# The linear stage's rounds: the place of the mask, of the second norm and of the gathers

## The reference

```python
qkv = x @ W_qkv.T
q, k, v = (to_heads(t) for t in jnp.split(qkv, 3, axis=-1))      # 16 heads of 8
q = softplus(q / norm(q)); k = softplus(k / norm(k))
kv = einsum('bhnd,bhnc->bhdc', k, v) * 8 ** -0.5
ksum = sum(k, axis=2) + 1e-6
out = einsum('bhnd,bhdc,bhn->bhnc', q, kv, 1 / einsum('bhnd,bhd->bhn', q, ksum))
```

## Time and profile before

| | us |
|---|---|
| median of 3 runs | 2046.47 |
| lowest and highest of them | 2041.81, 2047.84 |
| the profiled execution | 2041.99 |
| its span, first to last instruction | 2040.3 |
| the linear stage in it | 910.0 to 1094.1 |

### The profile page before, as it was taken

How to read it: one execution, slowest core, us unless ns; L and a number is a source line. 1 busy time by engine, 2 the same in 40 slices (tenths; PEclk the granted TensorE clock), 3 DMA queues, 4 the chain that set the end, 5 groups by cost and what they waited for, 6 DMA issues and landing times. The chain is left out here.

```text
span 2040.3 us, 25722 instructions
## 1 busy us (share of the span) xinstructions
PE 1580.5 (77%) x8391; PEld 826.9 (41%) x8391; DVE 1224.0 (60%) x2794; ACT 1069.7 (52%) x2129; POOL 800.5 (39%) x1497
## 2 busy tenths in 40 slices
PE   2899999992659885074772595289999999789998
PEld 1133333320436554063662463123333333367776
DVE  3788888875743323004656750778888888334553
ACT  2377777774333333034663331257777777545553
POOL 3455555416243333515634376614444431011220
PEclk7699999996755555596765698579999999989999
DMA  4122222200000002100004122211111111000000
GB/s 117 66 66 66 65 67 64 64 14 1 1 0 1 0 1 88 54 28 10 3 1 129 55 39 30 90 48 60 61 62 59 61 64 45 26 18 11 11 6 16
DMA packets 84968, 85.16 MB, mean 42 GB/s; under 512 B 35942, under 2 KB 67536, under 8 KB 84708
## 3 DMA queue, kind: packets, MB, share of 16 engines
q1 hardware_dynamic: 73914, 75.14, 11.4%
q0 software_dynamic: 7680, 6.06, 1.8%
q10 hardware_dynamic: 3242, 2.32, 0.4%
HBM read 59.76 MB, written 25.17 MB: 42 GB/s over the span
## 5 line engine op out<-in xcount | busy, mean ns | idle before, releaser
L942 DVE TENSOR_REDUCE arena<-psum 128x2 f32<-128x1024 f32 x512 | 601.6, 1216 | 102.8 <-PE psum L727 98.3
L839 ACT ACTIVATE arena<-psum 128x512 f32<-128x512 f32 x1024 | 553.5, 595 | 135.4 <-PE psum L740 127.4
L727 PE MATMUL psum<-arena 72*128 72x512 bf16 x1024 | 287.8, 397 | 46.4 <-DMA arena<-L_k_parts 17.8
L740 PE MATMUL psum<-arena 99*128 99x512 bf16 x1024 | 312.0, 386 | 10.6 <-issue 7.1
L750 PE MATMUL psum<-arena 128*32 128x512 f32 x2048 | 274.5, 608 | 3.0 <-ACT arena L839 1.9
L2543 ACT ACTIVATE arena<-arena 128x128 f32<-128x128 f32 x316 | 128.6, 481 | 133.5 <-POOL arena L2520 121.3
L740 PEld LDWEIGHTS psum<-arena 99*128 99x128 bf16 x1024 | 74.6, 98 | 287.5 <-ACT arena L839 222.1
L2514 POOL TENSOR_SCALAR arena<-arena 128x4 f32<-128x4 f32 x112 | 30.6, 273 | 368.7 <-DVE arena L2508 363.2
L727 PEld LDWEIGHTS psum<-arena 72*128 72x128 bf16 x1024 | 95.3, 99 | 189.9 <-DVE arena L942 29.0
L2505 DVE BATCH_NORM_STATS2 arena<-arena 128x6 f32<-128x128 f32 x448 | 96.7, 278 | 75.9 <-PEq L101 21.0
L636 POOL TENSOR_TENSOR arena<-arena 128x16 bf16<-128x16 f32 x64 | 14.3, 223 | 290.8 <-DVE arena L942 218.4
(11 more groups left out here) (433 smaller groups left out, 2532.2 us busy)
## 6 DMA issues: line engine op xcount, KB each, us to landing
arena<-L_q_parts SPq DMA_DIRECT2D x192, 96.0 KB
arena<-L_k_parts SPq DMA_DIRECT2D x180, 96.0 KB
L_q_parts<-arena SPq DMA_DIRECT2D x16, 384.0 KB, 3.4
L_k_parts<-arena SPq DMA_DIRECT2D x16, 384.0 KB, 3.3
arena<-in_L_ffn_w SPq DMA_DIRECT2D x1, 2048.0 KB, 10.6
ec_result<-arena SPq DMA_DIRECT2D x1, 2048.0 KB, 9.7
arena<-in_L_ffn_fc2s SPq DMA_DIRECT2D x1, 2048.0 KB, 16.1
ec_normed<-arena SPq DMA_DIRECT2D x2, 1024.0 KB, 7.3
```

Of the source, the lines that this page charges most:

```text
L727: last = nc.tensor.matmul(bank[:, 512 * h:512 * h + 512], columns(q9[0:QK_ROWS], i, m // 2, 128 * (2 * (m % 2) + h), 128), columns(k9[0:QK ...
L740: nc.tensor.matmul(acts.bank(name), columns(k9[0:ROWS], i, g, 128 * k, 128), columns(q9[0:ROWS], i, g, 0, 512), start=True, stop=True).the ...
L839: nc.scalar.activation(prob[:, k % 2, g, :], acts.bank(name), ACT.Exp, scale=scale).then_inc(act_taken, 1)
L942: nc.vector.tensor_reduce(neg_max[:, i % 2, 2 * m:2 * m + 2], maxes.bank(("max", i, m)).rearrange("p (h t) -> p h t", h=2), axis=AX.X, op= ...
```

## The change

Three edits, all in the order of calls inside a round. On GpSimd, `of_x4.factors(pool, i)` now stands ahead of the gathers of batch i+2 and no longer behind them. On ScalarE, `of_x5.apply` of batch i-4 stands ahead of `copy(i-1)` and `turn(i-2)`; it stood behind both, directly ahead of `copy_tokens` for the same batch, which stays last. On VectorE, the mask of batch i-2 was the last call of round i; now the mask of batch i-3 is the first call of round i. No instruction is added, removed or resized, and TensorE's list is as it was.

```diff
--- before.py
+++ after.py
@@ -1800,10 +1800,10 @@
                     of_o4.factors(pool, i)
                 if inside(i - 3):
                     of_o5.factors(pool, i - 3)
+                if inside(i):
+                    of_x4.factors(pool, i)
                 if inside(i + FETCH_AHEAD):
                     fetch(pool, i + FETCH_AHEAD, fetched[i + FETCH_AHEAD])
-                if inside(i):
-                    of_x4.factors(pool, i)
                 if inside(i - 3):
                     of_x5.factors(pool, i - 3)
             pool.wait_ge(of_o4.factors_done, B)
@@ -1933,12 +1933,13 @@
                     copy_tokens(i - 1, turned4, copied4)
                 if inside(i - 2):
                     soften(i - 2)
+                if inside(i - 4):
+                    of_x5.apply(act, c.n, c.x, i - 4)
                 if inside(i - 1):
                     copy(i - 1)
                 if inside(i - 2):
                     turn(i - 2)
                 if inside(i - 4):
-                    of_x5.apply(act, c.n, c.x, i - 4)
                     copy_tokens(i - 4, turned5, copied5)
 
         @block.vector
@@ -1985,6 +1986,8 @@
             dve.wait_ge(masks, 4)
             dve.wait_ge(ones_set, 1)
             for i in range(LAST_ROUND):
+                if inside(i - 3):
+                    mask(i - 3)
                 if inside(i - 2):
                     scale(i - 2)
                 if inside(i):
@@ -2008,8 +2011,6 @@
                 if inside(i - 3):
                     dve.wait_ge(added5, TPB * (i - 2))
                     of_x5.spread(dve, c.x, i - 3)
-                if inside(i - 2):
-                    mask(i - 2)
 
 
 BITS = 30
```

## The result

The changed kernel takes 2033.65 us, the median of 5 runs (2028.81 to 2035.66), against 2042.03 for 5 runs of the kernel before (2041.81 to 2047.84): ratio 0.9950, 95% interval 0.9931 to 0.9968. That is 8.4 us faster by the medians and 10.2 by the ratio. I had forecast 2041.4 us, 5 us faster, with a range that ends at 2036.5. The direction was right, the forecast gain about half of what came, and the time lies outside the range. Part of the miss in time is its base: the sum starts from 2046.47 us, the median of three runs of the kernel before, which with two more runs became 2042.03.

A forecast was written before the change was run, and what follows sets the result against it. No engine is full; a 17.5 us loop of waits bounds the linear stage. Terms of -3.1 (gathers) and -1.95 us (norm in the tail), off the 2046.47 us median, gave 2041.4 us, range 2036.5 to 2046.0.

The forecast's parts named there:

- The loop: Full round of the linear stage: TensorE 6.2 + ScalarE 0.7 + TensorE 4.6 + VectorE 6.05 = 17.5 us.
- The mask edit: VectorE, end of one round to head of the next: same stream of instructions and waits, 0.0 us.
- Gathers: GpSimd at the stage's start: x4's factors of batch 0 no longer wait behind batch 2's gathers, -3.1 us.
- The norm in full laps: ScalarE, full rounds: x5's norm ahead of the evacuation makes the square some 0.2 us late, hidden; 0 us.
- in the tail: Round 8: batch 7's inverse norm comes earlier, so its output starts right behind its mask, -1.95 us.
- The base of the sum: Forecast gain of 5.05 us set against the timed runs' median, 2046.47 us, 4.5 us above the profiled run.
- TensorE's clock: TensorE's laps: up to 1.2 us each depends on when the clock rises; taken as zero, plus or minus 2 us.
- the merged pause: TensorE ahead of output: 2.33 + 1.80 us become one pause of 4.1, speaking against the change; sum left as is.
- Rival 1: Denser TensorE work gains clock, before batch 7's output and in two laps: about -8.5 us, 2038; chance 0.36.
- Rival 2: Gathers in front of o4's factors on GpSimd make VectorE's addition late: total -2.8 us, 2043.7; chance 0.13.
- Rival 3: Longer TensorE pause costs clock in outputs and projections, 5.9 us: total +0.9 us, 2047.4; chance 0.07.
- rival 4: The change does nothing because the loop holds the stage's head too: 2046 us; chance 0.04.

The follow-up runs named there:

- the transposes put back: Changed kernel without the mask edit, plus a TensorE wait for VectorE's bounded squares ahead of x5's transposes in rounds 4 to 8: ratio 0.9977.
- The filler run: Kernel before, plus four extra float32 products on TensorE in round 8 between the sums and x5's transposes: ratio 0.9992.
- the last version: Kernel with the mask behind x4's statistics, plus ScalarE's x4 norm ahead of the inverse norm and token copy ahead of exp: 2017.84 us, ratio 0.9885.
- the early mask: Changed kernel with the mask placed behind x4's statistics, ahead of o5's addition, squares and x5's statistics: 2023.22 us, ratio 0.9911.
- the filler through the laps: Gathers and norm edits, plus eight extra float32 products behind TensorE's work in rounds 2 to 9: 2027.24 us, ratio 0.9918.

## Why the prediction failed, step by step

**The loop.** Right. The laps stayed at 17.4 to 17.5 us in the middle, TensorE's output still waited for the mask (4.33 us, undivided, as forecast), and moving the mask for real took 10 us off. That bears out 17.5 as the sum of those four terms.

**The mask edit: 0.** Right: the lists are the same, and the run alone gave 1.0000.

**Gathers: -3.1.** Right: x4's factors came 3.14 us earlier and the head is 3.43 shorter. The first value copy at 939.02 for 939.0 is in part luck, as the stage had begun 0.37 later and the projection was faster. Against the three other traces with the old head (31.26 to 31.37) the gain is 2.8 us, and the run alone gave -2.7.

**The norm in full laps: 0; in the tail: -1.95.** In the full laps the period stayed (17.54 and 17.42 us in the middle, for 17.54 and 17.53). In the tail the mechanism and its size were right (-1.96). The inverse norm of batch 7 now starts 0.43 us behind ScalarE's last work, waiting for VectorE's squares and for nothing else:

```profile
1056.16 0.31 ACT L1897 ACTIVATE arena<-arena 128x128 f32<-128x128 f32 x1 [0.43 <-DVE arena L1978]
```

It is a row of ScalarE's timeline of the changed kernel and answers to the earlier trace rows.

**The base of the sum: 2046.47 us.** This step failed. The forecast gain was taken off the median of three runs, 4.5 us above the profiled one. Five runs give 2042.03, and the later groups of 25, 15 and 16 runs give 2041.87, 2042.41 and 2041.50. From 2042.03 the same gain makes 2037.0. Of the 7.8 us between 2041.4 and 2033.65, 4.4 are the base and 3.3 the gain.

**TensorE's clock: "I take zero and plus or minus 2 us".** This step failed too, and it is the one of the mechanism. What the runs showed in its place is -3.3 us in the tail and about -1 in the laps (-1.2 against the trace of before, -0.7 to -1.1 against the other three with the old head). I had looked at the pause of an inner lap, seen that the clock falls there in any case, and carried that to round 8, where it had just risen inside the sums. There, where the transposes stand decides. Round 7 with the transposes put back is one pair that shows it. The other, for round 8, is the norm alone against the mask edit alone: their laps agree to 0.1 us, the sums begin alike (1.43 us for eight products, where the clock rises inside), and only the transposes differ. TensorE with the norm moved:

```profile
1057.53 1.43 PE L1845 MATMUL psum<-arena 128*128 128x129 f32 x8
1058.79 0.60 PE L1850 MATMUL psum<-arena 128*128 128x128 f32 x4
1059.23 0.60 PE L1820 MATMUL psum<-arena 128*128 128x128 f32 x4
1062.66 0.40 PE L1859 MATMUL psum<-arena 128*128 128x16 f32 x2 [2.83 <-DVE arena L1956]
```

and with the instructions of the kernel before:

```profile
1058.31 1.43 PE L1845 MATMUL psum<-arena 128*128 128x129 f32 x8
1059.58 0.60 PE L1850 MATMUL psum<-arena 128*128 128x128 f32 x4
1062.49 1.08 PE L1820 MATMUL psum<-arena 128*128 128x128 f32 x4 [2.31 <-ACT arena L2543]
1063.45 0.61 PE L1859 MATMUL psum<-arena 128*128 128x16 f32 x2
```

The same work directly behind the sums, and then one longer pause, leaves the next output at 2.4 GHz; divided, with the transposes 2.3 us later, they themselves already run at 1.2 GHz (1.08 for 0.60). The filler run, which keeps the divided order but fills the first gap, agrees. This is shown where the clock rises inside the sums; where it had risen before them, the divided pause left the start of output 6 at 2.4 GHz as well. So I had the sign of the merged pause wrong here: a pause of 2.83 us left the output at 2.4 GHz, one of 2.31 us with the transposes behind it did not.

The Trainium skill, "TensorE: Matmul & The Clock Gate", section "HAM oscillation — how this bites in real kernels", says that waits between bursts throttle the clock again and again. The full laps agree: behind a pause of 4.33 us the output starts at 1.2 GHz (0.61 us for its first row). I had applied the rule to the pause alone and not to the work ahead of it.

**The rivals.** Rival 1 (denser work in the tail gains clock, about 2038) was what came, for nearly its reason. Its total came close in part by luck: it left out output 6 (-1.73), had output 7 right (-1.6), and counted two faster projections (-2.4), where the laps gave about half of that, by a faster output. Its prices also add up to -9.05 and not to -8.5, and a spread of 2 us about -5.05 runs from -3.05 to -7.05 and not from -3.8 to -6.1. I held it back with "through the whole tail the clock never rose". That is not so even in the trace of before, where 0.85 was granted from the last values to mask 6; it holds behind that (0.50), and is no evidence for the changed kernel. Rival 2 (o4's factors make the addition late) showed in small in the changed kernel, 0.5 us at the first copy of values, and in full once the laps got shorter: it sets the 14.85 us of the last version. Rival 3 had the wrong sign; rival 4 held for the mask alone.

**What stays open.** Output 7 at 2.4 GHz (1.58 us): it was so in the three traces with the ScalarE edit and no more on TensorE or in the laps (2.09 us), and in the four with the early mask or the filler through the laps (2.0 to 2.1). It was not so with the filler in the tail alone and not with the late transposes, though the work ahead of it looked alike in the latter. I can name the edit, not the cause. The same holds for the lap at whose end the projection misses the rise (18.5 us; the seventh lap before, the sixth after and with the gathers alone).

## What to carry to other kernels

Where an engine with two clock levels sits in a dependency loop, price a move of its short bursts by the work that they adjoin, stretch by stretch; the answer of one lap doesn't hold for another in which the clock has just risen. Look for what a second late engine hides: the fast output was worth 0.5 us with the late inverse norm and 1.7 us without. And compare the engine's list of instructions before pricing a move by a loop's edge: from the end of a round to the head of the next is no move at all, while the same three instructions placed ahead of o5's addition, the squares and x5's statistics gave 10 us. When the laps get shorter, look at every chain again: the place of the gathers cost almost nothing at 17.5 us a lap and sets the lap at 14.85.

## What the runs showed of the hardware

The pattern of the granted clock repeated between traces to a degree that I had not expected: the tail of the kernel before was 36.97 and 36.96 us in two traces, that with the ScalarE edit 31.68, 31.70 and 31.69 in three (the laps moved by 0.5 us between such traces), and the lap of 18.50 us was the last one in all four traces with the old head (before, norm alone, mask alone, filler in the tail). With filler products outputs ran at 2.4 GHz wholly or in part (2.0 to 2.6 us for 3.8), yet the projection after a wait of 1.62 us began at 1.2 GHz again (1.22 us for a pair).
